# The start of the local layers: tile 0's shift column ahead of the table products, and tile 0's sine products and sum ahead of its power on POOL

## The chip, the cores and the metric

One core of a Trainium2 chip runs the whole program in one launch. The metric is the device time of an execution in microseconds; a profiled execution also gives a trace. The engines are TensorE (PE; PEld is its weight load), VectorE (DVE), ScalarE (ACT), GpSimd (POOL) and SyncE (SP), which here issues all DMAs. They work from queues of their own and meet by semaphores.

## The reference

The input x has 4 sequences of 1024 tokens with 128 features, in float32. The reference adds to x the normalised output of a latent attention (16 heads), and to the result the normalised output of a network of two "local layers", whose input is the normalised x. The change touches the first half of a local layer only:

```python
h = shift_token(x)                    # features 64..127 come from the token before
q, k, v = split(h @ wqkv)             # 8 heads of 64
q, k = l2norm(q) * qs, l2norm(k) * ksc
q = q * cos * scale + rotate_half(q) * sin * scale
k = k * cos / scale + rotate_half(k) * sin / scale
o = local_attention(q, k, v)          # windows of 64, this one and the one before
x = x + o @ wo
```

Behind it stands an MLP with a shift, a norm and a gate, and then the next layer, with other weights.

## The kernel before

**Stages.** `latent_attention_and_window_layers` calls `project`, `attend`, `mix`, then for each of the two layers `window` and `mlp`, and at the end `last_norm`. Each stage is a block in which every engine has a program of its own, written out in full; a new block starts when all engines have ended the last one. The residual stream `xf_sb` stays in SBUF throughout.

**`window`.** It works on 32 tiles (`NT`) of 128 tokens. `w_hT` holds a tile transposed, twice over, with one column more than tokens: its upper 64 partitions are written one column to the right, which makes the shift by a token, and column 0 of that half has to be filled from the last column of the tile before (times zero where a sequence starts). The function `carry` does this on DVE (L1120). For tile 0 it reads a column that a memset has set to zero.

**The path of a tile t.** TensorE turns it (`turn_x`, L891) and ScalarE copies it to `w_hT` in two pieces (L1001, L1003). TensorE projects queries and keys to PSUM (`project_qk`, L899) once copy and shift column are there, and values (`project_v`, L903). ScalarE copies queries and keys to `w_raw` (`copy_raw`, L1008) and squares them (L1013). DVE multiplies the PSUM values by the cosine table (`cosines`, L1134), and sums the squares by head (`sums`: L1125 and, with the floor, L1129, giving `w_ssm`). POOL makes the inverse root of these sums as a power with exponent -0.5 (`norms`, L1089, 128x16), and, in `rotate`, four products of `w_raw` with the sine table (L1079) and the sum of cosine and sine parts, `w_rot` (L1084). The norm commutes with the rotation, so DVE multiplies `w_rot` by the inverse roots at the end (`normalise`, L1143). TensorE turns the result (L911), ScalarE and DVE copy it to `w_qT` and `w_kT` (L1024, L1147), TensorE makes the scores (L917, L930), and so on through maxima (L1155), exponentials (L1031), division (L1168), turns, values (L954) and the output projection (L961).

**The order.** Each engine goes through slots s = -2 to 34, and in each slot does the steps of several tiles in an order written by hand (`slot`). In DVE's, the order is normalise(s-1), divide(s-2), carry(s+2), copy_kT(s-1), residual(s-3), cosines(s+1), maxima(s-1), copy_pT(s-2), maxima(s-1), sums(s+1). POOL has no slots: it does `norms` and `rotate` of each tile in turn. SP spreads the values of each tile with two DMAs (L877, L878), and starts with that after all four memsets.

**The start of a layer.** Before its first slot, DVE does four memsets (the shift column's source in `w_hT`, the left edges of `w_kT` and `w_vb0`, the floor of the square sums), which raise the semaphore `zeroed`, and six products that make the layer's cosine and sine tables from the given ones and the layer's scales (L1107, L1111), which raise `tables`. ScalarE waits for all four memsets before its first slot, POOL for all six products.

Of the kernel before, what the change touches and what calls it, by code (L numbers as in the profile page):

```python
# [20 lines left out]
ALU = mybir.AluOpType  # L21
# [4 lines left out]
P = 128  # L26
NT = B * S // P
TB = S // P
# [14 lines left out]
DEPTH, HEADS, DH, WIN = 2, 8, 64, 64  # L43
# [607 lines left out]
WINDOW_LOADS = 16 * (4 + 4 * DEPTH)  # L651
# [160 lines left out]
def window(nc, io, sb, layer):  # L812
# [6 lines left out]
    with ExitStack() as ctx:  # L819
# [7 lines left out]
        cos, sin = tile("w_cos", [P, TB, 2, DH]), tile("w_sin", [P, TB, 2, DH])  # L827
        hT = tile("w_hT", [P, 2, P + 1])
# [166 lines left out]
        def _(act):  # L995
# [67 lines left out]
                if runs(s - 2):  # L1063
                    copy_oT(s - 2, (s - 2) % 4)

            act.wait_ge(zeroed, layer * 4 + 4)
            slots(act, slot)

        @block.gpsimd
        def _(pool):  # L1070
            def rotate(t, r):

                at_least(pool, raw_done, base, t, 1)
                at_least(pool, rot_done, base, t, 0)
                out, src = (x.rearrange("p (w h u d) -> p w h u d", w=2, h=HEADS, u=2) for x in (t2[:, :], raw[:, r % 2, :]))
                for half in range(2):
                    for w in range(2):
                        tab = sin[:, t % TB, w, half * 32:half * 32 + 32].unsqueeze(1).broadcast_to((P, HEADS, 32))
                        i = pool.tensor_tensor(out[:, w, :, half, :], src[:, w, :, 1 - half, :], tab, ALU.mult)  # L1079
                i.then_inc(t2_done, 1)  # L1080
                at_least(pool, t1_done, base, t, 1)
                at_least(pool, t2_done, base, t, 1)
                at_least(pool, qkT_done, base, t, -1)
                pool.tensor_tensor(rot[:, r % 2, :], t1[:, r % 2, :], t2[:, :], ALU.add).then_inc(rot_done, 1)  # L1084

            def norms(t, r):
                at_least(pool, ssm_done, base, t, 1)
                at_least(pool, unit_done, base, t, -1)
                pool.tensor_tensor(rn[:, r % 2, :], ssm[:, r % 2, :], sb["mhalf"][:, 0:16], ALU.pow).then_inc(rn_done, 1)  # L1089

            pool.wait_ge(tables, layer * 6 + 6)
            for t in range(NT):
                norms(t, t % 4)
                rotate(t, t % 4)

        @block.vector
        def _(dve):

            dve.memset(hT[WIN:P, 1, P:P + 1], 0.0).then_inc(zeroed, 1)
            dve.memset(kT[:, :, :, 0:WIN], 0.0).then_inc(zeroed, 1)  # L1100
            dve.memset(vb[0][0:WIN, :], 0.0).then_inc(zeroed, 1)
            dve.memset(ss[:, :, :, 1], 1e-24).then_inc(zeroed, 1)

            dve.wait_ge(w_in, WINDOW_LOADS)
            for w in range(2):
                sc = sb["scales"][:, bass.ds(layer, 1), w, :].broadcast_to((P, TB, DH))
                dve.tensor_tensor(cos[:, :, w, :], sb["cos"][:, :, w, :], sc, ALU.mult).then_inc(tables, 1)  # L1107
                for half in range(2):
                    sc = sb["scales"][:, bass.ds(layer, 1), w, 32 - 32 * half:64 - 32 * half].broadcast_to((P, TB, 32))
                    part = slice(32 * half, 32 * half + 32)  # L1110
                    dve.tensor_tensor(sin[:, :, w, part], sb["sin"][:, :, w, part], sc, ALU.mult).then_inc(tables, 1)  # L1111
            dve.wait_ge(zeroed, layer * 4 + 4)
            dve.wait_ge(tables, layer * 6 + 6)

            def carry(t, r):

# [6 lines left out]
            def sums(t, r):  # L1123
                at_least(dve, sq_done, base, t, 1)
                dve.tensor_reduce(ss[:, r % 2, :, 0], sq[:, :].rearrange("p (h d) -> p h d", d=DH), AX.X, ALU.add).then_inc(ss_done, 1)  # L1125
                at_least(dve, ss_done, base, t, 1)
                at_least(dve, rn_done, base, t, -1)

                dve.tensor_reduce(ssm[:, r % 2, :], ss[:, r % 2, :, :], AX.X, ALU.max).then_inc(ssm_done, 1)  # L1129
# [44 lines left out]
            def slot(s):  # L1174
                def runs(t):
                    return 0 <= t < NT
                if runs(s - 1):
                    normalise(s - 1, (s - 1) % 4)
                if runs(s - 2):
                    divide(s - 2, (s - 2) % 4)  # L1180
                if runs(s + 2):
                    carry(s + 2, (s + 2) % 4)
                if runs(s - 1):
                    copy_kT(s - 1, (s - 1) % 4)
                if runs(s - 3):
                    residual(s - 3, (s - 3) % 4)
                if runs(s + 1):
                    cosines(s + 1, (s + 1) % 4)
                if runs(s - 1):
                    maxima(s - 1, (s - 1) % 4, 0)  # L1190
                if runs(s - 2):
                    copy_pT(s - 2, (s - 2) % 4)
                if runs(s - 1):
                    maxima(s - 1, (s - 1) % 4, 1)
                if runs(s + 1):
                    sums(s + 1, (s + 1) % 4)

            slots(dve, slot)

# [345 lines left out]
```

## Time and profile before

Three executions took 1448.87, 1451.42 and 1455.66 us; the median is 1451.42. The profiled execution took 1451.36 us, of which the traced span is 1449.6 us.

| Engine | busy us in the span | share |
|---|---|---|
| TensorE, matmuls | 1268.6 | 88% |
| DVE | 1129.5 | 78% |
| ScalarE | 930.0 | 64% |
| POOL | 705.3 | 49% |

| Stretch, us from the span's start | what runs | POOL busy us |
|---|---|---|
| 616 to 927 | `window` of layer 0 | 269.87 |
| 927 to 1020 | `mlp` of layer 0 | 9.66 |
| 1020 to 1331 | `window` of layer 1 | 269.98 |
| 1331 to 1422.9 | `mlp` of layer 1 | 9.66 |
| 1422.9 to 1449.6 | `last_norm` | 9.66 |

A profile's busy time is that in which an engine works on an instruction; waiting for a semaphore is idle time. The share of an engine over the whole span says little here, since POOL works in some stages only. A row of the timeline gives the start, the duration, the engine, the line, the operation with output and inputs, and in brackets the idle time before it with what ended it. The start of a row that shows no idle time can lie some hundredths of a microsecond before the end of the row before it on the same engine.

### The profile page before, as it was taken

How to read it: one execution, taken by the hardware profiler on the slowest of the kernel's cores; microseconds unless marked ns; L12 is line 12 of the kernel's file. 1: busy time of each engine (PE TensorE's matmuls, PEld its weight loads, DVE VectorE, ACT ScalarE, POOL GpSimd, SP SyncE). 2: the span in 40 equal slices, each digit the busy share in tenths (PEclk: the TensorE clock that was granted, in tenths of full speed). 3: DMA queues.
4: the chain of work that ended last, by engine and by line, in shares of the span. 5: the costliest groups of instructions: out<-in, count | busy, mean ns of one | idle time of the engine just before them, and what ended most of it. 6: DMA issues, size and time to landing. Idle time of an engine off the chain costs nothing. (4 is left out here: it accounts for less than half of the span.)

```text
span 1449.6 us, 30335 instructions
## 1 busy us (share of the span) xinstructions
PE 1268.6 (88%) x10501; PEld 718.9 (50%) x10501; DVE 1129.5 (78%) x2980; ACT 930.0 (64%) x2597; POOL 705.3 (49%) x742
## 2 busy tenths in 40 slices
PE   4689999999999997369999999699599999996991
PEld 2323333333343333336666666565366666665551
DVE  5788888888888861669899998566599989995667
ACT  4437777776777674748888887232488888883320
POOL 1011222122212221469999999110599999992102
PEclk9859999999999998579999999799899999998896
DMA  4431111111112002001211111000012111110001
GB/s 112 134 104 50 56 42 38 40 59 44 38 38 60 14 5 84 18 23 31 51 31 31 31 33 36 1 1 1 15 33 55 31 31 31 31 31 9 1 1 58
DMA packets 35055, 55.45 MB, mean 38 GB/s; under 512 B 6978, under 2 KB 22732, under 8 KB 32588
## 3 DMA queue, kind: packets, MB, share of 16 engines
q1 hardware_dynamic: 34328, 53.37, 14.0%
q8 instruction: 85, 1.39, 0.4%
q14 instruction: 66, 0.54, 0.1%
q10 hardware_dynamic: 576, 0.15, 0.1%
HBM read 26.77 MB, written 8.39 MB: 24 GB/s over the span
## 5 line engine op out<-in xcount | busy, mean ns | idle before, releaser
L516 ACT ACTIVATE a_prob<-a_psE 128x512 f32<-128x512 f32 (+3 forms) x768 | 318.3, 500 | 140.5 <-PE a_psE L444 137.9
L444 PE MATMUL a_psE<-a_qs,a_ks 84*128 84x512 bf16 (+3 forms) x768 | 248.3, 336 | 17.4 <-ACT a_prob L516 8.3
L599 DVE CUSTOM_DVE_ANT_0 a_psM<-a_psM,mask_q 128x384 f32<-128x384 f32 (+3 forms) x512 | 242.4, 507 | 18.6 <-PE a_psM L432 18.0
L432 PE MATMUL a_psM<-a_ks,a_qs 72*128 72x512 bf16 (+3 forms) x768 | 250.3, 343 | 5.7 <-PEq L86 3.2
L1089 POOL TENSOR_TENSOR w_rn<-w_ssm,mhalf 128x16 f32<-128x16 f32 x64 | 213.6, 3337 | 66.7 <-DVE w_ssm L1129 66.7
L551 POOL TENSOR_SCALAR_AFFINE_SELECT a_prob<-a_prob 128x512 f32<-128x512 f32 x128 | 81.1, 634 | 332.5 <-ACT a_prob L516 307.9
L601 DVE TENSOR_REDUCE a_nm<-a_psM 128x1 f32<-128x512 f32 x256 | 175.8, 687 | 46.6 <-PE a_psM L432 46.6
L1031 ACT ACTIVATE w_prob<-w_psS,w_bias 128x128 f32<-128x128 f32 x512 | 179.8, 376 | 21.4 <-DVE w_bias L1155 21.2
L1079 POOL TENSOR_TENSOR w_t<-w_raw,w_sin 128x256 f32<-128x256 f32 x256 | 178.6, 729 | 0.0
L444 PEld LDWEIGHTS a_psE<-a_qs,a_ks 84*128 84x128 bf16 x768 | 74.5, 98 | 180.3 <-ACT a_prob L516 97.1
L1084 POOL TENSOR_TENSOR w_rot<-w_t 128x1024 f32<-128x1024 f32 x64 | 150.9, 2358 | 8.8 <-issue 0.4
L458 PE MATMUL a_psO<-a_prob,v_all 128*32 128x512 f32 (+3 forms) x1536 | 148.4, 503 | 0.0
L899 PE MATMUL w_psQK<-w_wqkv,w_hT 128*128 128x512 f32 x256 | 124.1, 608 | 9.3 <-DVE w_t L1134 5.6
L1031 ACT ACTIVATION_READ_ACCUMULATOR w_prob<-w_psS,w_bias 128x1 f32 x512 | 110.6, 216 | 0.0
L1155 DVE TENSOR_REDUCE w_bias<-w_psS 128x4 f32<-128x512 f32 x128 | 87.7, 687 | 26.8 <-PE w_psS L930 26.8
L432 PEld LDWEIGHTS a_psM<-a_ks,a_qs 72*128 72x128 bf16 x768 | 76.4, 100 | 57.2 <-DVE a_nm L599 18.5
L1143 DVE TENSOR_TENSOR w_rot<-w_rot,w_rn 128x1024 f32<-128x1024 f32 x64 | 78.1, 1221 | 29.2 <-POOL w_rot L1084 29.2
L911 PE MATMUL w_psT<-ident,w_rot 128*128 128x128 f32 x512 | 70.8, 283 | 29.9 <-DVE w_rot L1143 27.1
L911 PEld LDWEIGHTS w_psT<-ident,w_rot 128*128 128x128 f32 x512 | 56.6, 144 | 75.5 <-DVE w_rot L1143 75.3
L1260 PE MATMUL f_psU<-f_hT,f_w 128*114 128x512 f32 (+1 forms) x192 | 88.8, 613 | 0.0
L1134 DVE TENSOR_TENSOR w_t<-w_psQK,w_cos 128x1024 f32<-128x1024 f32 x64 | 78.0, 1219 | 12.9 <-ACT w_raw L1008 12.7
L1038 ACT ACTIVATE w_pT<-w_psT 128x512 f32<-128x512 f32 x64 | 38.2, 598 | 73.4 <-PE w_psT L939 73.4
(136 smaller groups left out, 2371.5 us busy)
## 6 DMA issues: line engine op xcount, KB each, us to landing
w_vb<-w_v SPq DMA_DIRECT2D x128, 128.0 KB, 2.3
a_qs<-q_parts SPq DMA_DIRECT2D x16, 576.0 KB
a_ks<-k_parts SPq DMA_DIRECT2D x16, 576.0 KB
q_parts<-p_parts SPq DMA_DIRECT2D x24, 128.0 KB
k_parts<-p_parts SPq DMA_DIRECT2D x24, 128.0 KB
out_x<-l_y SPq DMA_DIRECT2D x8, 256.0 KB, 2.3
a_qs<-a_nmT SPq DMA_DIRECT2D x32, 48.0 KB
w_wqkv<-in_wqkv SPq DMA_DIRECT2D x2, 768.0 KB, 7.4
```

Source lines behind the costliest of these rows:

```text
L432: pe.matmul(out, qs[0:ROWS, g, j, i * P:(i + 1) * P], ks[0:ROWS, g, j, 512 * kc:512 * kc + n], start=True, stop=True).then_inc(m_ready, 1)
L444: pe.matmul(psE[:, r % NRING, 0:w], ks[0:KROWS, g, j, kt * P:(kt + 1) * P], qs[0:KROWS, g, j, q0:q0 + w], start=True, stop=True).then_inc( ...
L458: mm = pe.matmul(psO[32 * j:32 * j + 32, q0:512], v_flat[:, col + j * VA:col + j * VA + 32], prob[G % NPROB][:, j, 0:512 - q0], start=(kt ...
L516: act.activation(prob[G % NPROB][:, j, 0:w], psE[:, r % NRING, 0:w], ACT.Exp, scale=SCALE0).then_inc(e_read, 1)
L599: dve.tensor_tensor_reduce(scores, scores, sb["mask_q"][:, 512 - n:512], -1.0, -3.0 * NEG, ALU.add, ALU.min, low).then_inc(m_read, 1)
L601: dve.tensor_reduce(low, scores, AX.X, ALU.max, negate=True).then_inc(m_read, 1)
L899: pe.matmul(psQK[:, w, :], hT[:, r % 2, 0:P], wqkv[:, bass.ds(layer * (3 * INNER) + w * INNER, INNER)], start=True, stop=True).then_inc(qk ...
L911: i = pe.transpose(psT[:, w, c * P:(c + 1) * P], rot[:, r % 2, w * INNER + c * P:w * INNER + (c + 1) * P], sb["ident"])
L1031: i = act.activation(prob[:, p, w, c, :], psS[:, w, c * P:(c + 1) * P], ACT.Exp, bias=bias[:, p, n:n + 1], accum_out=den[:, p, n:n + 1])
L1079: i = pool.tensor_tensor(out[:, w, :, half, :], src[:, w, :, 1 - half, :], tab, ALU.mult)
L1084: pool.tensor_tensor(rot[:, r % 2, :], t1[:, r % 2, :], t2[:, :], ALU.add).then_inc(rot_done, 1)
L1089: pool.tensor_tensor(rn[:, r % 2, :], ssm[:, r % 2, :], sb["mhalf"][:, 0:16], ALU.pow).then_inc(rn_done, 1)
```

## The change

In both local layers:

- ScalarE starts its slots once one memset is done, not four.
- DVE does one memset (the source of the shift column), waits for it, and does the shift column of tile 0 at once; then the other three memsets and the six table products. Its slots follow, in which the column of tile 0 is left out.
- POOL does `rotate` of tile 0 first and `norms` of tile 0 after it. From tile 1 on it is `norms`, then `rotate`, as before.

Nothing that is computed changes.

```diff
-            act.wait_ge(zeroed, layer * 4 + 4)
+            act.wait_ge(zeroed, layer * 4 + 1)
             slots(act, slot)
...
             pool.wait_ge(tables, layer * 6 + 6)
-            for t in range(NT):
+            rotate(0, 0)
+            norms(0, 0)
+            for t in range(1, NT):
                 norms(t, t % 4)
                 rotate(t, t % 4)
...
-                if runs(s + 2):
+                if runs(s + 2) and s > -2:
                     carry(s + 2, (s + 2) % 4)
...
+            dve.memset(hT[WIN:P, 1, P:P + 1], 0.0).then_inc(zeroed, 1)
+            dve.wait_ge(zeroed, layer * 4 + 1)
+            dve.wait_ge(w_in, WINDOW_LOADS)
+            carry(0, 0)
+            dve.memset(kT[:, :, :, 0:WIN], 0.0).then_inc(zeroed, 1)
+            dve.memset(vb[0][0:WIN, :], 0.0).then_inc(zeroed, 1)
+            dve.memset(ss[:, :, :, 1], 1e-24).then_inc(zeroed, 1)
```

Behind these lines come the six products and the two waits on `zeroed` and `tables`, as they were; the whole piece stands behind the definitions of the steps now.

## Rows read from the trace of the kernel before

**Rows 1.** Mid-layer stretch: length, busy us of PE, PEld, DVE, ACT, POOL; clock, DMA.
```profile
662.80:680.50 17.70, 17.28 (x195) 11.96 (x194) 16.06 (x25) 14.74 (x49) 16.94 (x12) 1.00 0.13 31
```

**Rows 2.** Timeline of layer 1, middle: start, duration, engine, line, operation.
```profile
1190.11 1.22 DVE L1143 TENSOR_TENSOR w_rot<-w_rot,w_rn 128x1024 f32<-128x1024 f32 x1
1190.27 3.82 POOL L1089 TENSOR_TENSOR w_rn<-w_ssm,mhalf 128x16 f32<-128x16 f32 x1 [0.54 <-DVE w_ssm L1129]
...
1199.30 2.91 POOL L1089 TENSOR_TENSOR w_rn<-w_ssm,mhalf 128x16 f32<-128x16 f32 x1
1199.45 1.23 DVE L1143 TENSOR_TENSOR w_rot<-w_rot,w_rn 128x1024 f32<-128x1024 f32 x1 [0.70 <-POOL w_rot L1084]
```

**Rows 3.** Timeline of the start of layer 0.
```profile
616.28 0.45 PE L891 MATMUL w_psT<-ident,xf_sb 128*128 128x128 f32 x1 [14.35 <-PEq L686]
616.30 0.06 DVE L1099 MEMSET w_hT<- 64x1 f32 x1 [2.04 <-PEq L686]
...
617.62 0.27 ACT L1001 ACTIVATE w_hT<-w_psT 64x128 f32<-64x128 f32 x1 [1.65 <-DVE w_ss L1102]
...
618.24 0.48 PE L891 MATMUL w_psT<-ident,xf_sb 128*128 128x128 f32 x1 [1.51 <-ACT w_hT L1003]
...
620.21 0.34 DVE L1120 TENSOR_SCALAR w_hT<-w_hT,carry 64x1 f32<-64x1 f32 x2
...
620.57 3.75 PE L899 MATMUL w_psQK<-w_wqkv,w_hT 128*128 128x512 f32 x4 [1.86 <-DVE w_hT L1120]
...
624.36 1.02 ACT L1008 ACTIVATE w_raw<-w_psQK 128x1024 f32<-128x1024 f32 x1 [3.29 <-PE w_psQK L899]
...
625.42 1.22 DVE L1134 TENSOR_TENSOR w_t<-w_psQK,w_cos 128x1024 f32<-128x1024 f32 x1 [4.87 <-ACT w_raw L1008]
...
626.79 1.95 PE L899 MATMUL w_psQK<-w_wqkv,w_hT 128*128 128x512 f32 x4 [1.10 <-DVE w_t L1134]
...
627.80 0.19 DVE L1129 TENSOR_REDUCE w_ssm<-w_ss 128x16 f32<-128x32 f32 x1
...
628.14 2.90 POOL L1089 TENSOR_TENSOR w_rn<-w_ssm,mhalf 128x16 f32<-128x16 f32 x1 [14.07 <-DVE w_ssm L1129]
...
631.00 2.77 POOL L1079 TENSOR_TENSOR w_t<-w_raw,w_sin 128x256 f32<-128x256 f32 x4
...
633.86 1.02 ACT L1008 ACTIVATE w_raw<-w_psQK 128x1024 f32<-128x1024 f32 x1 [1.91 <-POOL w_t L1079]
633.92 2.34 POOL L1084 TENSOR_TENSOR w_rot<-w_t 128x1024 f32<-128x1024 f32 x1
636.22 2.91 POOL L1089 TENSOR_TENSOR w_rn<-w_ssm,mhalf 128x16 f32<-128x16 f32 x1
636.36 1.22 DVE L1143 TENSOR_TENSOR w_rot<-w_rot,w_rn 128x1024 f32<-128x1024 f32 x1 [3.96 <-POOL w_rot L1084]
...
644.94 1.22 DVE L1143 TENSOR_TENSOR w_rot<-w_rot,w_rn 128x1024 f32<-128x1024 f32 x1
```

**Rows 4.** Timeline of the start of layer 1.
```profile
1028.14 1.02 ACT L1008 ACTIVATE w_raw<-w_psQK 128x1024 f32<-128x1024 f32 x1 [3.07 <-PE w_psQK L899]
...
1040.14 1.23 DVE L1143 TENSOR_TENSOR w_rot<-w_rot,w_rn 128x1024 f32<-128x1024 f32 x1 [3.95 <-POOL w_rot L1084]
...
1048.26 1.23 DVE L1143 TENSOR_TENSOR w_rot<-w_rot,w_rn 128x1024 f32<-128x1024 f32 x1
```

**Rows 5.** TensorE in stretches: busy, granted clock, DMA share, GB/s.
```profile
620.00:625.00 5.00, 4.43 (x6) 0.50 0.00 0
625.50:635.00 9.50, 5.06 (x12) 1.00 0.24 55
636.00:642.00 6.00, 4.34 (x39) 0.50 0.00 0
```

**Rows 6.** Timeline of layer 0's end: the normalisations of tiles 30 and 31.
```profile
902.46 1.23 DVE L1143 TENSOR_TENSOR w_rot<-w_rot,w_rn 128x1024 f32<-128x1024 f32 x1 [0.72 <-POOL w_rot L1084]
...
911.12 1.22 DVE L1143 TENSOR_TENSOR w_rot<-w_rot,w_rn 128x1024 f32<-128x1024 f32 x1
```

More of the change, by code:

```diff
@@ L1097, in _ @@
         def _(dve):
[L1099 to L1113, printed above, removed]
             def carry(t, r):
@@ L1196, in slot @@
                     sums(s + 1, (s + 1) % 4)
+            dve.memset(hT[WIN:P, 1, P:P + 1], 0.0).then_inc(zeroed, 1)
[5 more added lines that the diff above has]
+            dve.memset(ss[:, :, :, 1], 1e-24).then_inc(zeroed, 1)
+            for w in range(2):
+                sc = sb["scales"][:, bass.ds(layer, 1), w, :].broadcast_to((P, TB, DH))
+                dve.tensor_tensor(cos[:, :, w, :], sb["cos"][:, :, w, :], sc, ALU.mult).then_inc(tables, 1)
+                for half in range(2):
+                    sc = sb["scales"][:, bass.ds(layer, 1), w, 32 - 32 * half:64 - 32 * half].broadcast_to((P, TB, 32))
+                    part = slice(32 * half, 32 * half + 32)
+                    dve.tensor_tensor(sin[:, :, w, part], sb["sin"][:, :, w, part], sc, ALU.mult).then_inc(tables, 1)
+            dve.wait_ge(zeroed, layer * 4 + 4)
+            dve.wait_ge(tables, layer * 6 + 6)
             slots(dve, slot)
```

## The prediction

> **What bounds the kernel now.** The kernel is a row of stages with a meeting of all engines between them, so I first cut the span by stage. The two window layers last some 311 us each, from 616.3 and from 1020.2. The chain of waits of the page covers only the last norm, behind the last such meeting, and says nothing of the layers; their order has to be read from the timeline.
>
> In the middle of a layer two tiles take 17.70 us and POOL is busy for 16.94 of them [rows 1]. POOL does three things per tile: the power (2.91 or 3.82 us) [rows 2], four sine products (2.77) and the sum (2.34) [rows 3]. Each even tile's power waits 0.54 us for the square sums that DVE has only just made; an odd one's starts at once [rows 2]. In return every second normalisation on DVE waits 0.70 us for POOL's sum. So POOL and DVE hold each other, and neither has slack that could swallow a late start or an early one: what the first tile gains should stay to the layer's last tile.
>
> Call N(t) the start of DVE's normalisation of tile t. It is the first thing DVE does in a slot, and TensorE's turns, the scores and the exponentials of the slot hang on it. In the middle of a layer N steps by 9.34 us from odd to even (1190.11 to 1199.45), and by 8.40 from even to odd, since two steps make the 17.7 us pair [rows 1, 2].
>
> The start of a layer is where the change sits [rows 3]. TensorE has turned tile 0 at 616.73, but ScalarE begins its copy at 617.62, put down to DVE's last memset. The next turn ends at 618.72, and TensorE then waits for DVE's shift column: it stands behind the memsets and the six table products, starts at 620.21, and lets the query and key projection start at 620.57. The raw copy follows at 624.36, the squares' sum and maximum end at 627.99, and only at 628.14 does POOL do its first piece, tile 0's power. Its sine products start at 631.00, 5.6 us after the raw tile lay there, and N(0) is 636.36. Layer 1 has the same distances: raw copy at 1028.14, N(0) at 1040.14, again 12.00 us later [rows 4].
>
> **The change, part by part.**
>
> *ScalarE's shorter wait.* It waits for one memset, which ends at 616.36, not four. Its first copy can start when the turn ends, at 616.73 + 0.05 = 616.78, not 617.62. The second turn followed the copy's start by 0.62 us, so it runs from 617.40 to 617.88. Nobody reads the three other memsets before DVE itself passes them in program order, or SP before its first spread of V, which needs V's copy, several us later.
>
> *The shift column of tile 0 first.* It adds one wait of DVE on its own memset, and moves one instruction, half of the 0.34 us pair [rows 3]: it is over by 616.8, so the projection starts behind the second turn, at about 617.90 instead of 620.57. Gain 2.67 us. The projection takes the same 3.75 us, at the low granted clock of 0.50 [rows 5], and ends at 621.65; the raw copy runs from 621.69 to 622.71. Queued behind the moved column are three memsets and six products. They end some 0.3 us later, near 620.5, and tile 1's column near 620.7. Nothing waits: the cosines of tile 0 need the raw tile of 622.71. That column and wait cost nothing while that cover of 2 us lasts. The cover for POOL's wait on the tables is the same.
>
> *POOL's new order for tile 0.* Sine products, sum, power. The sine products need the raw tile and the tables: from 622.8, 2.77 us, to 625.6. The sum starts 0.15 later and ends at 625.72 + 2.34 = 628.06. It needs the cosines, which DVE makes from 622.75 to 623.97 (raw copy plus 1.22): there. The power starts at 628.0; the maximum of the square sums is ready by 622.71 + 2.61 = 625.3 (before: 625.38 to 627.99): there. It ends at 630.92, and N(0) waits for it instead of for the sum: about 631.0. Gain of N(0): 636.36 - 631.0 = 5.35 us, of which 2.67 is the column's and 2.7 the order's (POOL no longer waits from the raw tile's end at 625.38 to 628.14). The work of POOL is the same, 8.0 us; it only begins earlier.
>
> *Who else is queued behind it.* ScalarE's raw copy of tile 2 waits for tile 0's sine products, which now end at 625.6 instead of 633.8: harmless. Is DVE free at 631.0? Tile 1: its projection may start when tile 0's cosines are done, 624.0, takes 1.95 (the same form at 626.79), and its raw copy runs 626.05 to 627.07; squares' maximum 2.61 later, 629.7. That is 1.2 us ahead of 630.9, when POOL wants it for tile 1's power. If TensorE were still at half clock there, the projection would take 3.9 us and POOL would lose 0.7. Tile 2's raw copy starts near 630.4, when before it was 633.86; its reader, DVE's third cosine piece, comes four us behind N(0). So what stands around N(0) is late by less than it was early.
>
> *What comes after N(0).* Before, POOL starts tile 1's power at 636.22 and DVE its normalisation at 636.36, both let go by the sum. After, both are let go by tile 0's power, at 630.9 and 631.0. The order on both engines from there is untouched.
>
> *The sum.* 5.35 us in layer 0 and the same in layer 1, as its distances are the same: 10.7 us. The profiled execution took 1451.36 us, 1.8 over its span and 0.1 below the median of 1451.42. The median less 10.7 is 1440.7, down 0.74%. About 0.5% (7.3 us) is what a measurement of this kernel can tell from no change.
>
> **A cost that the trace shows elsewhere.** The power takes 3.82 us when DVE's normalisation has begun just before it (1190.11, then 1190.27), and ends 2.76 us after that normalisation ends; it takes 2.91 when POOL is first by 0.15 (1199.30, then 1199.45) [rows 2]. So POOL's read is held off while DVE reads two SBUF operands. In the new start POOL's second power is queued on POOL itself and DVE's normalisation hears a semaphore, so I expect POOL first, as at 636.22; but the lead of 0.14 us there follows a sum, and behind a power the trace has no such pair. Bounds: nothing lost, or 1 us a layer as in rival 1. I take nothing, the nearer row.
>
> The Trainium skill has this lock (SBUF — State Buffer, "SBUF: two separate sides"): the instruction that starts first, if VectorE's reads two SBUF inputs against a GpSimd one, keeps the shared pair to its end and the other stands still. The blocked power agrees; the other half does not, since the normalisation that starts 0.15 behind a power takes 1.23 and not 2.9 us more. By the rule both kernels would lose alike there, and the sum would stay.
>
> **Rivals.**
>
> *1. The normalisation wins the lock at tile 1 (0.18).* The power of tile 1 is then the long one: N(1) is N(0) + 9.34 instead of + 8.58 (636.36 to 644.94), or + 8.12 in layer 1 [rows 3, 4]. From there odd and even change roles. The next step is 8.40 for 9.34, so most of it is back two tiles on, but the layer's last step, N(30) to N(31), becomes 9.34 where it is 8.66 now [rows 6]. Layer 0 loses 0.76 - 0.94 + 0.68 = 0.5, layer 1, whose first step was 0.46 shorter, 1.0. Gain 10.7 - 1.5 = 9.2, time 1442.2. For it: both events are released by one instruction. The rule of the skill cited above says who suffers here, not who is first.
>
> *2. TensorE keeps its clock (0.15).* Before, it stood idle before N(0)'s turns and fell to the low level, 0.50 from 636 to 642, after 1.00 until 635 [rows 5]. After, the idle time is 630.3 to 632.3, half as long. If the clock stays at 1.00, DVE's slot no longer ends last; then POOL's 8.1 us does, and N(1) is N(0) + 8.2. The next power then starts before N(1), and odd and even change roles one step later, which is worth up to the 0.94 by which the steps differ, less 0.68 at the layer's end. Layer 0: 0.4 + 0.94 - 0.68 = 0.7; layer 1, whose first step is short already, 0.2. Gain 11.6, time 1439.8.
>
> *3. Half is lost (0.08).* One part frees POOL but the other is held by something the trace does not show, such as tile 1's sums late by over 2 us, so only the column's 2.67 or the order's 2.7 a layer arrives: 5.3 us, 1446.1. Against it are the 1.2 us and 2 us of cover above.
>
> *4. Nothing happens (0.04).* ScalarE or TensorE still starts late, or a layer's end is not tied to its start. 1451. Against it: POOL is idle for 0.76 us in 17.70 [rows 1].
>
> *5. Slower (0.05).* Every power becomes a long one. That needs DVE to be ready for the next normalisation before each power, so its slot would have to beat POOL's 9.3 us and still be first at every tile. Each step would be 9.34 instead of 8.87 on average: 0.47 x 31 x 2 = 29 us more, less 10.7: 1470. It decides at the point where POOL waits for the square sums at every tile; today it waits at each second one, and after a long power POOL is the late one, which corrects it. So it is unlikely.
>
> **How the numbers follow.** The forecast has 0.50, and its time is 1440.7. Faster by over 0.5%: forecast, rivals 1 and 2, 0.83. Within 0.5%: rivals 3 and 4, 0.12. Slower: 0.05. The range takes in rivals 1 and 2 and, on either side, some 2 us by which a median of these runs (1448.87 to 1455.66) may stand off: 1436.5 to 1444.5; the 0.17 of rivals 3 to 5 stay outside.
>
> **What would show it.** The timeline of the changed kernel: the first projection at 1.6 to 1.7 us after the first turn (now 4.3), at once behind the second turn. POOL's first instruction of a layer a sine product, 6.5 us after the first turn and 0.1 behind the raw copy; the power with no idle time before it. N(0) 14.7 us after the first turn instead of 20.1, put down to POOL's power. The last normalisation of each layer about 5.3 us nearer to the layer's start, and the MLPs and the last norm unchanged in length. Tile 1's power 2.91 us if the forecast holds, 3.8 to 4.0 for rival 1; the clock between N(0) and N(1) for rival 2. The prediction is wrong if N(31) - N(0) grows by over 2 us, or if POOL idles between its power of tile 0 and that of tile 1.

## The result, and the profile after

The changed kernel took 1444.21 us (median of 4 executions, 1443.88 to 1445.37), the kernel before 1453.24 on the same chip (4, 1448.87 to 1455.66): ratio 0.9945, 95% interval 0.9921 to 0.9969. Two repeats, with more executions beside them, gave 0.9946 (0.9930 to 0.9962) and 0.9936 (0.9913 to 0.9958). It is faster by 8 to 9 us where 10.7 were forecast, and 1444.2 stands 3.5 us over the forecast time of 1440.7. The forecast started from a median of 1451.4 in three executions, and the same kernel's median is 1453.2 in four: by that alone the forecast time would be 1442.5, and 1.7 us are left.

The page of the changed kernel's profiled execution (1445.37 us), its span and two groups:

```profile
span 1443.6 us, 30337 instructions
...
L1089 POOL TENSOR_TENSOR w_rn<-w_ssm,mhalf 128x16 f32<-128x16 f32 x64 | 213.7, 3340 | 16.7 <-DVE w_ssm L1115 16.7
...
L1079 POOL TENSOR_TENSOR w_t<-w_raw,w_sin 128x256 f32<-128x256 f32 x256 | 178.7, 731 | 39.3 <-ACT w_raw L1008 39.3
```

Before, POOL's power had 66.7 us of idle time ahead of it and the sine products none: POOL now comes to a layer's first tile with the sine products. Line numbers have moved: normalise is L1129, the shift column L1106, the square sums' maximum L1115, the cosines L1120.

The start of layer 0, timeline of the changed kernel (start, duration, engine, line), beside [rows 3]:

```profile
620.18 0.45 PE L891 MATMUL w_psT<-ident,xf_sb 128*128 128x128 f32 x1 [14.35 <-PEq L686]
620.21 0.06 DVE L1184 MEMSET w_hT<- 64x1 f32 x1 [2.04 <-PEq L686]
620.30 0.21 DVE L1106 TENSOR_SCALAR w_hT<-w_hT,carry 64x1 f32<-64x1 f32 x1
...
620.73 0.27 ACT L1001 ACTIVATE w_hT<-w_psT 64x128 f32<-64x128 f32 x1 [0.85 <-PE w_psT L891]
...
621.60 3.62 PE L899 MATMUL w_psQK<-w_wqkv,w_hT 128*128 128x512 f32 x4
...
625.26 1.02 ACT L1008 ACTIVATE w_raw<-w_psQK 128x1024 f32<-128x1024 f32 x1 [2.85 <-PE w_psQK L899]
...
626.43 2.78 POOL L1079 TENSOR_TENSOR w_t<-w_raw,w_sin 128x256 f32<-128x256 f32 x4 [8.46 <-ACT w_raw L1008]
...
629.36 2.35 POOL L1084 TENSOR_TENSOR w_rot<-w_t 128x1024 f32<-128x1024 f32 x1
...
631.67 5.78 POOL L1089 TENSOR_TENSOR w_rn<-w_ssm,mhalf 128x16 f32<-128x16 f32 x2
...
634.61 1.23 DVE L1129 TENSOR_TENSOR w_rot<-w_rot,w_rn 128x1024 f32<-128x1024 f32 x1 [1.31 <-POOL w_rn L1089]
```

The column lies right behind its memset, the projection starts 1.4 us behind the first turn (4.3 before), POOL begins with the sine products 0.15 us behind the raw copy, and N(0) stands 14.40 us behind the first memset, 20.06 before. The powers of tiles 0 and 1 take 5.78 us together: 2.9 each, neither is blocked.

The layer as a whole is best read from a few distances. N(t) is the start of DVE's normalisation of tile t, as in the prediction; M is the layer's first memset, E the first memset of the MLP behind it. All are from the timelines of the profiled executions, in us. Rows below those of the two repeats belong to the experiments, which come later; "filled" are those with added turns on TensorE.

| Kernel, layer | N(0)-M | N(1)-N(0) | N(2)-N(1) | N(30)-N(0) | N(31)-N(30) | E-N(31) | E-M |
|---|---|---|---|---|---|---|---|
| before, 0 | 20.06 | 8.58 | 9.35 | 266.10 | 8.66 | 17.07 | 311.89 |
| before, 1 | 19.84 | 8.12 | 9.36 | 265.66 | 8.69 | 17.07 | 311.26 |
| changed, 0 | 14.40 | 8.17 | 8.12 | 264.52 | 9.31 | 18.51 | 306.74 |
| changed, 1 | 13.87 | 8.16 | 9.28 | 266.03 | 9.59 | 18.51 | 308.00 |
| repeat, 0 | 14.42 | 8.17 | 9.21 | 265.60 | 9.31 | 18.54 | 307.87 |
| repeat, 1 | 13.91 | 8.18 | 9.29 | 266.00 | 9.61 | 18.53 | 308.05 |
| second repeat, 0 | 14.10 | 8.17 | 9.31 | 265.75 | 9.31 | 18.44 | 307.60 |
| second repeat, 1 | 13.88 | 8.19 | 9.26 | 266.06 | 9.59 | 18.53 | 308.06 |
| column alone, 0 | 16.57 | 8.12 | 9.34 | 265.70 | 8.68 | 17.33 | 308.28 |
| column alone, 1 | 16.54 | 8.11 | 9.35 | 265.04 | 9.60 | 19.11 | 310.29 |
| order alone, 0 | 17.25 | 8.18 | 9.37 | 265.74 | 9.31 | 18.46 | 310.76 |
| order alone, 1 | 17.20 | 8.18 | 9.37 | 265.75 | 9.60 | 18.40 | 310.95 |
| memset at tile 4, 0 | 14.41 | 8.18 | 9.20 | 266.60 | 8.66 | 16.86 | 306.53 |
| memset at tile 4, 1 | 14.04 | 8.18 | 9.35 | 266.13 | 9.31 | 18.41 | 307.89 |
| before, memset at tile 5, 0 | 20.07 | 8.11 | 8.27 | 264.50 | 9.31 | 18.20 | 312.08 |
| before, memset at tile 5, 1 | 20.06 | 8.10 | 8.41 | 264.62 | 9.31 | 19.05 | 313.04 |
| filled, slot 32, 0 | 14.41 | 8.18 | 8.12 | 264.59 | 9.33 | 15.63 | 303.96 |
| filled, slot 32, 1 | 14.28 | 8.18 | 9.20 | 265.98 | 9.60 | 16.69 | 306.55 |
| filled, slots 32, 33, 0 | 14.41 | 8.18 | 8.11 | 264.55 | 9.34 | 15.64 | 303.94 |
| filled, slots 32, 33, 1 | 13.75 | 8.18 | 9.21 | 266.00 | 9.62 | 15.63 | 305.00 |
| filled, slots 2, 32, 33, 0 | 14.40 | 8.18 | 8.12 | 264.43 | 9.33 | 15.63 | 303.79 |
| filled, slots 2, 32, 33, 1 | 12.99 | 9.33 | 8.11 | 265.93 | 9.61 | 15.63 | 304.16 |

N(0) comes 5.6 to 6.0 us earlier in a layer, and the two stages together are only 7.2 to 8.4 us shorter. From N(0) on, the layer has become longer by 0.5 to 1.7 us (layer 0) and 2.7 to 2.8 us (layer 1). Behind N(30) alone it is 2.0 to 2.4 us longer in every one of these layers; in layer 0 the stretch from N(0) to N(30) has become shorter, in layer 1 longer by 0.3 to 0.4. The rest of the span is outside the change: the instructions ahead of layer 0 are the same, and yet M of layer 0 lay between 613.9 and 620.2 us in the profiled executions. The profile that was predicted from had 616.3, the changed kernel's 620.2; that is why the spans differ by only 6.0 us although the two stages are 8.4 shorter.

### The profile page after: what moved, and what is told of

It reads as the page before. It is cut to its first block and busy times, and to the rows that moved or that the text cites. A ratio compares the mean times of both kernels' runs of the same rounds, so it can differ in the third digit from the quotient of the medians.

```text
span 1443.6 us, 30337 instructions
## 1 busy us (share of the span) xinstructions
PE 1267.0 (88%) x10501; PEld 717.8 (50%) x10501; DVE 1129.8 (78%) x2980; ACT 930.5 (64%) x2597; POOL 705.5 (49%) x742
## 3 DMA queue, kind: packets, MB, share of 16 engines
HBM read 26.77 MB, written 8.39 MB: 24 GB/s over the span
## 5 line engine op out<-in xcount | busy, mean ns | idle before, releaser
L432 PEld LDWEIGHTS a_psM<-a_ks,a_qs 72*128 72x128 bf16 x768 | 76.4, 100 | 57.1 <-DVE a_nm L599 18.5
L1129 DVE TENSOR_TENSOR w_rot<-w_rot,w_rn 128x1024 f32<-128x1024 f32 x64 | 78.2, 1221 | 29.7 <-POOL w_rot L1084 27.1
L899 PEld LDWEIGHTS w_psQK<-w_wqkv,w_hT 128*128 128x128 f32 x256 | 49.2, 194 | 68.4 <-issue 68.4
```

The costliest lines, as they stand in the source:

```text
L432: pe.matmul(out, qs[0:ROWS, g, j, i * P:(i + 1) * P], ks[0:ROWS, g, j, 512 * kc:512 * kc + n], start=True, stop=True).then_inc(m_ready, 1)
L899: pe.matmul(psQK[:, w, :], hT[:, r % 2, 0:P], wqkv[:, bass.ds(layer * (3 * INNER) + w * INNER, INNER)], start=True, stop=True).then_inc(qk ...
```

## The experiments

Two theories were held against each other. **"Roles"**: the start gain arrives in full, and the layer's end takes part of it back, since the long power (3.82 us, DVE's normalisation ahead of it) has passed from even to odd tiles [rows 2, 6]. **"Wear"**: the gain is used up along the layer. The "long power" is the one of 3.82 us; a tile "has" it when its own power is the long one.

### Each part alone

```diff
  # "column": the changed kernel with POOL's old order
-            rotate(0, 0)
-            norms(0, 0)
-            for t in range(1, NT):
+            for t in range(NT):
```

> The changed kernel with POOL's old order for tile 0 (power first): the column's part alone. Both theories: the first projection starts 2.7 us earlier, the raw copy, POOL's power and N(0) too, so N(0) stands 17.4 us behind the layer's first memset (before 20.06 and 19.84, changed kernel 14.40 and 13.87). Theory 'roles' (a start gain arrives in full, and a layer's end takes some 2.1 us back if the long power has passed from even to odd tiles): nothing makes POOL's first steps other than in the kernel before, but TensorE's idle time before the first normalisation is as long as there, so even tiles keep the long power, the end from N(31) to the next stage is 17.07 us and each window stage is 2.7 us shorter, 5.4 in all: ratio 0.996. Theory 'wear' (a start gain is used up along the layer whatever the order): the stages are less than 2 us shorter and the loss stands between N(1) and N(30).

```diff
  # "order": the kernel before with POOL's new order for tile 0
-            for t in range(NT):
+            rotate(0, 0)
+            norms(0, 0)
+            for t in range(1, NT):
```

> The kernel before with tile 0's sine products and sum in front of its power: the order's part alone. Both: the raw copy stays where it was, N(0) comes 2.7 to 2.9 us earlier, 17.2 us behind the first memset. Theory 'roles': TensorE stands idle for 2 us before N(0)'s turns as in the changed kernel, keeps its clock, N(1) comes 8.2 us behind N(0), the long power passes to odd tiles at least in layer 0, and the step N(30) to N(31) is 9.3 and the end 18.5 us there: the stage is 2.7 + 0.4 + 0.9 - 2.1 = about 2 us shorter. If the even tiles keep it, 2.8 us. Ratio 0.996 to 0.998. Theory 'wear': under 2 us in both layers whoever has the long power.

Timelines of layer 0; M is 616.95 with the column alone, 614.31 with the order alone. First the column's:

```profile
625.31 2.90 POOL L1089 TENSOR_TENSOR w_rn<-w_ssm,mhalf 128x16 f32<-128x16 f32 x1 [10.59 <-DVE w_ssm L1113]
...
633.52 1.22 DVE L1127 TENSOR_TENSOR w_rot<-w_rot,w_rn 128x1024 f32<-128x1024 f32 x1 [3.95 <-POOL w_rot L1084]
```

The order's:

```profile
623.38 2.77 POOL L1079 TENSOR_TENSOR w_t<-w_raw,w_sin 128x256 f32<-128x256 f32 x4 [11.31 <-ACT w_raw L1008]
...
631.56 1.23 DVE L1145 TENSOR_TENSOR w_rot<-w_rot,w_rn 128x1024 f32<-128x1024 f32 x1 [1.30 <-POOL w_rn L1089]
```

N(0)-M is 16.5 to 16.6 with the column, 0.8 better than expected, and 17.2 with the order, as expected. The column's surplus is TensorE's: its first projection took 3.15 us in layer 0 of this run, 3.75 before. Ratios: column 0.9973 (0.9957 to 0.9990), order 0.9985 (0.9969 to 1.0001). By stages, the column gives 3.6 and 1.0 us, the order 1.1 and 0.3. The column was expected to give 5.4 in all and gave 4.6; the order, expected at 2 to 2.8 a layer, gave less, and its interval reaches 1, so by times alone it cannot be told from no change. The table shows where the difference to N(0)'s gain went: layer 0 of the column kept the long power on even tiles and has an end of 8.68 + 17.33; the other three layers ended with it on the odd ones, at 27.8 to 28.7 us from N(30) to E, where layer 0 of the column has 26.0 and the kernel before 25.7 to 25.8. Against "wear": N(30) - N(0) is 265.0 to 265.8 us in all four, and 265.7 to 266.1 in the kernel before.

The roles can also pass late. In layer 1 of the column's run the steps alternate in the old way to tile 28; then one is 8.71 instead of 8.39, and from there the order is turned. In layer 1 of the changed kernel the same step has 0.35 us too much (9.69 for 9.34): DVE stands idle though POOL's sum is done. What holds it there is open. This step is too long by 0.3 us or more in layer 1 of every kernel of these runs that has the moved column and keeps POOL's old order from tile 1 to tile 30, and in neither layer of the kernels without the moved column; so it comes with that part of the change.

### The changed kernel again

> The changed kernel once more, as the measure for the others of this call and for how much the stages ahead of the first window stage differ from one profiled execution to the next. Both theories: window stages 306.7 and 308.0 us. If the 3.9 us by which the first window stage began later in the changed kernel's profile are chance, this one begins within 616 to 621 at another place.

> The changed kernel on the same chip as the two others of this call, as their measure. Layer stages 306.7 to 308.1 us, ends of 18.5 us.

M of layer 0 was 618.4 and 618.8, the stages 307.9 and 308.1, then 307.6 and 308.1 us. In both, N(2) - N(1) is 9.2 to 9.3 in both layers, where the first profile had 8.12 in layer 0. So the first profile shows the better of two courses there.

### Passing the long power back

```diff
             for t in range(1, NT):
+                if t == 2:
+                    pool.memset(pspare[:, :], 0.0)
                 norms(t, t % 4)
```

> The changed kernel with one more POOL instruction, a memset of 128x512 to a tile that nobody reads, between tile 1's sum and tile 2's power, in both layers. It delays the power of tile 2 by about 0.4 us, so that the normalisation of tile 1 is first. Theory 'roles': tile 2's power then takes 3.8 to 4.2 us instead of 2.91, N(2) comes about 9.4 us behind N(1) (changed kernel 8.12 and 9.28), the long power stays with the even tiles to the end, the step N(30) to N(31) is 8.66 instead of 9.31 and 9.59, and from N(31) to the next stage 17.07 us instead of 18.51. Added work makes the kernel faster: layer 0 by 2.1 - 1.25 = 0.9 us, layer 1 by about 2.4 - 0 = 2.4 us, in sum 3 us below the changed kernel. Theory 'wear': the added work costs 0.4 to 1.6 us a layer and the end stays at 18.5 us.

This missed: the end stayed at 18.4 and the ratio was 0.9952 (0.9933 to 0.9971). The added memset did make tile 2's power long (3.67 us), but N(2) to N(3) was long too, 9.33 us, so that the alternation came out as without it. The step behind N(1) was 9.2 to 9.3 in the changed kernel already, since DVE's slot and not POOL set it. The cause is in the clock, below. The second attempt put the memset where the steps had settled:

```diff
             for t in range(1, NT):
+                if t == 4:
+                    pool.memset(pspare[:, :], 0.0)
                 norms(t, t % 4)
```

> The changed kernel with one more POOL instruction, a memset of 128x512 to a tile that nobody reads (0.52 us where it was tried before), this time ahead of tile 4's power, where the steps have settled (before, ahead of tile 2's, both engines still ran through TensorE's low clock and the long power fell on tile 3 as well). Theory 'roles' (a layer's end costs 2.1 us more when odd tiles have the long power): tile 4's power becomes long, N(3) to N(4) is 9.35 instead of 8.39, and from there even tiles have the long power: N(30) to N(31) 8.7 instead of 9.3 to 9.6, from N(31) to the next stage 17.1 to 17.3 us instead of 18.5. The stage is 1.0 us longer ahead and 2.1 shorter behind: about 306.8 us against 307.9 in layer 0 and 308.0 in layer 1, in spite of added work. Theory 'wear': the added work costs 0.5 to 1.5 us a layer and the end stays at 18.5: 308.5 to 309.5 us.

Timeline of layer 0 with it, tile 4 and the layer's end:

```profile
656.51 0.53 POOL L1097 MEMSET w_pspare<- 128x512 f32 x1
656.68 1.23 DVE L1132 TENSOR_TENSOR w_rot<-w_rot,w_rn 128x1024 f32<-128x1024 f32 x1 [0.70 <-POOL w_rot L1085]
657.00 3.68 POOL L1090 TENSOR_TENSOR w_rn<-w_ssm,mhalf 128x16 f32<-128x16 f32 x1
...
666.04 1.23 DVE L1132 TENSOR_TENSOR w_rot<-w_rot,w_rn 128x1024 f32<-128x1024 f32 x1 [0.89 <-POOL w_rot L1085]
...
905.21 1.22 DVE L1132 TENSOR_TENSOR w_rot<-w_rot,w_rn 128x1024 f32<-128x1024 f32 x1
...
922.07 0.54 DVE L1358 MEMSET f_last<- 128x576 f32 x1 [0.47 <-PEq L819]
```

The normalisation starts 0.3 us ahead of the power, the power takes 3.68 us, and the step is 9.36 instead of 8.39. At the other end N(31) to E is 16.86 us where the changed kernel had 18.5, and N(30) to N(31) 8.66 where it had 9.31. The stage is 306.53 us, 1.1 to 1.3 below the two repeats, with half a microsecond of work added on POOL. (The changed kernel's first profile has 306.74 there, but with the short step behind N(1), 8.12; here that step was 9.20.) "Wear" is out for this layer. In layer 1 the steps alternated in the way of before up to tile 28, then came 8.72 for 8.39, and the end was the long one again, 9.31 + 18.41. The ratio 0.9947 (0.9928 to 0.9966) cannot tell 1 us from nothing; the timeline does.

The converse, on the kernel before:

```diff
             for t in range(NT):
+                if t == 5:
+                    pool.memset(pspare[:, :], 0.0)
                 norms(t, t % 4)
```

> The kernel before with one more POOL instruction, the memset of 128x512 to a tile that nobody reads, between tile 4's sum and tile 5's power: the converse of the run that put it ahead of tile 4's power in the changed kernel. Theory 'roles': it makes tile 5's power the long one, N(4) to N(5) is 9.35 instead of 8.39, and from there odd tiles have it: N(30) to N(31) 9.3 instead of 8.66, from N(31) to the next stage 18.5 instead of 17.07. 0.5 us of added work cost 0.95 + 0.65 + 1.44 = 3 us a layer: stages of 314.9 and 314.3 us against 311.9 and 311.3, 6 us in all, ratio 1.004. Theory 'no roles' (the changed kernel's long ends come from its other start in another way): 0.5 to 1 us a layer and an end of 17.07.

This missed too. In the profiled execution the steps of layer 0 began 8.11, 8.27, 9.34 and not 8.58, 9.35, 8.38 as in the kernel before: the odd tiles had the long power before the memset was reached, and the memset filled a time in which POOL would have waited for the square sums. The ends, from N(30) to E, were 27.5 and 28.4 us, as wherever the odd tiles have it, and the stages 312.1 and 313.0. So the run does not price a turn in mid-layer; it shows that the kernel before can come into either course by itself. The ratio was 1.0000 (0.9986 to 1.0015).

### TensorE's clock at the layer's end

```diff
  # "warm": s == NT; "warm2": s in (NT, NT + 1); at the start of TensorE's slot
+                if s in (NT, NT + 1):
+                    at_least(pe, raw_done, base, NT - 1, 1)
+                    at_least(pe, t1_done, base, NT - 1, 1)
+                    for _ in range(16):
+                        pe.transpose(psQK[:, 0, 0:P], sb["ident"], sb["ident"])
```

> The changed kernel with 16 turns of the identity into a free PSUM bank, whose results nobody reads, that TensorE makes at the start of its second last but two slot, ahead of the turns of tile 31, in both layers. It tells what of the layer's longer end is TensorE's low granted clock. Theory 'roles': N(30) to N(31) stays 9.3 to 9.6, as POOL sets it; TensorE no longer stands idle for 3.3 us, so its clock stays 1.00, the eight turns take 1.09 instead of 1.97 and the output projection 1.06 instead of 1.61, and from N(31) to the next stage it is 17.1 us or less instead of 18.5: stages of about 306.5 us. Rival (the end is longer for another cause, the order of DVE's and ScalarE's steps): the end stays at 18.4 or more whatever the clock.

> The changed kernel with 16 turns of the identity, whose results nobody reads, at the start of TensorE's slots 32 and 33, in both layers; the run with those of slot 32 alone had ends of 15.63 and 16.69 us, and in the second TensorE's clock fell while it waited 2.15 us for ScalarE. Theory 'roles and clock': both ends are 15.6 us, 2.9 below the changed kernel's 18.5, layer stages of 304 to 305.5 us, and the kernel is 6 to 8 us below the changed one: 1437 to 1439 us, ratio 0.990. Rival: the second filling delays the output projection of tile 30, 0.5 to 1 us worse than slot 32 alone.

The changed kernel at the end of layer 0, timeline:

```profile
899.13 1.22 DVE L1129 TENSOR_TENSOR w_rot<-w_rot,w_rn 128x1024 f32<-128x1024 f32 x1
899.29 3.82 POOL L1089 TENSOR_TENSOR w_rn<-w_ssm,mhalf 128x16 f32<-128x16 f32 x1 [0.53 <-DVE w_ssm L1115]
...
908.44 1.23 DVE L1129 TENSOR_TENSOR w_rot<-w_rot,w_rn 128x1024 f32<-128x1024 f32 x1 [2.20 <-POOL w_rot L1084]
...
909.72 1.97 PE L911 MATMUL w_psT<-ident,w_rot 128*128 128x128 f32 x8 [3.34 <-DVE w_rot L1129]
...
911.48 1.61 PE L961 MATMUL w_psO<-w_wo,w_oT 128*128 128x128 f32 x8
```

Its TensorE in two stretches (length, busy, granted clock, DMA):

```profile
899.00:908.00 9.00, 5.84 (x91) 1.00 0.13 31
908.50:912.50 4.00, 2.78 (x13) 0.59 0.00 0
```

The kernel before at the same place:

```profile
909.00:915.00 6.00, 4.74 (x67) 1.00 0.01 3
922.00:924.00 2.00, 2.00 (x16) 0.50 0.04 8
```

With slots 32 and 33 filled, timeline:

```profile
900.06 1.97 PE L971 MATMUL w_psQK<-ident 128*128 128x128 f32 x16
903.49 1.09 PE L911 MATMUL w_psT<-ident,w_rot 128*128 128x128 f32 x8 [1.46 <-DVE w_rot L1134]
904.42 1.06 PE L961 MATMUL w_psO<-w_wo,w_oT 128*128 128x128 f32 x8
```

and its TensorE:

```profile
903.20:908.00 4.80, 4.51 (x60) 1.00 0.00 0
```

Tile 31's power is the long one, so DVE waits 2.20 us for POOL and TensorE 3.34 us for DVE; then TensorE's eight turns take 1.97 us and the projection 1.61, at half clock. Filled, they take 1.09 and 1.06. N(31) to E falls from 18.5 to 15.63 (layer 0) and 16.69 (layer 1) with slot 32 alone, and to 15.64 and 15.63 with slot 33 too, below the 17.07 of the kernel before. In that kernel TensorE was at half clock in one stretch of the end, near 922, behind 2.14 us of waiting for ScalarE; in the changed kernel in two, and with both slots filled in none: 17.07, 18.51 and 15.63. N(30) to N(31) stays 9.3 to 9.6: that part is POOL's. So both added microseconds of the end have their cause: 0.65 to 0.9 from the long power, 1.44 from the clock. Slot 32 alone ran at 1440.03 us, ratio 0.9914 (0.9889 to 0.9938); both at 1439.03, 0.9910 (0.9892 to 0.9927).

### The low clock at the layer's start

Layer 1 of the changed kernel, timeline of the slot behind N(1):

```profile
1039.94 1.23 DVE L1129 TENSOR_TENSOR w_rot<-w_rot,w_rn 128x1024 f32<-128x1024 f32 x1 [1.11 <-POOL w_rot L1084]
...
1041.22 1.09 PE L911 MATMUL w_psT<-ident,w_rot 128*128 128x128 f32 x8 [2.25 <-DVE w_rot L1129]
...
1044.11 1.88 PE L930 MATMUL w_psS<-w_kT,w_qT 64*64 64x128 f32 x32
...
1049.22 1.22 DVE L1129 TENSOR_TENSOR w_rot<-w_rot,w_rn 128x1024 f32<-128x1024 f32 x1
```

TensorE there:

```profile
1033.08:1034.78 1.70, 1.51 (x10) 1.00 0.00 0
1034.50:1038.00 3.50, 3.06 (x39) 1.00 0.00 0
1038.00:1041.50 3.50, 1.25 (x6) 1.00 0.02 5
1042.50:1045.00 2.50, 2.43 (x22) 0.50 0.31 71
1046.00:1048.00 2.00, 2.00 (x37) 1.00 0.00 0
```

The clock is 1.00 for tile 0's turns (1033.07 on), as rival 2 had it, and falls one slot later, behind the 2.25 us in which TensorE waits for N(1). The scores take 1.88 us instead of 1.10, and the step is 9.28 instead of 8.12. In layer 0 of the same execution TensorE waited the same 2.25 us and the clock stayed at 1.00: that is the short step of 8.12. What decides between the two is open. In the kernel before, the low clock fell into the slot before [rows 5], where it cost at most 0.4 us. A last kernel fills this place too:

```diff
+                if s == 2:
+                    for _ in range(16):
+                        pe.transpose(psO[:, 0:P], sb["ident"], sb["ident"])
```

> The kernel with the fillings of slots 32 and 33, and 16 turns of the identity more at the start of slot 2, ahead of the turns of tile 1, in both layers. In the changed kernel TensorE stands idle for 2.2 us there, its clock falls to 0.50 in the slot, and the step from N(1) to N(2) is 9.2 to 9.3 us in seven of the eight layers seen with both parts of the change, 8.12 in the others. Theory 'the low clock has moved by one slot': with the filling the clock stays 1.00, the step is 8.1 us in both layers, N(30) - N(0) 264.5 us instead of 265.6 to 266.0, the long power stays with the odd tiles, and the layers are 1.1 to 1.5 us shorter than with slots 32 and 33 alone: stages of 304 us in both (warm2: 303.94, where the step was short by chance, and 305.00). Rival (DVE or ScalarE sets the step): it stays at 9.2 in at least one layer, with the clock at 1.00.

(Of all layers run with both parts and nothing added at the start, N(2) - N(1) was short (8.1) in 3 and long (9.2 to 9.35) in 11; the count in the expectation was of too few.) The step was 8.12 and 8.11, the stages 303.79 and 304.16 us, N(30) - N(0) 264.43 in layer 0 but 265.93 in layer 1. There the first projection ran at the full clock from the start. Timeline of layer 1, M at 1010.04:

```profile
1011.19 1.89 PE L899 MATMUL w_psQK<-w_wqkv,w_hT 128*128 128x512 f32 x4
1013.12 1.02 ACT L1016 ACTIVATE w_raw<-w_psQK 128x1024 f32<-128x1024 f32 x1 [1.17 <-PE w_psQK L899]
1014.33 2.77 POOL L1087 TENSOR_TENSOR w_t<-w_raw,w_sin 128x256 f32<-128x256 f32 x4 [29.47 <-DVE w_sin L1206]
...
1015.96 3.49 PE L899 MATMUL w_psQK<-w_wqkv,w_hT 128*128 128x512 f32 x4 [1.91 <-DVE w_t L1128]
```

The projection takes 1.89 us, and the prediction's cover is gone: POOL waits for the sine tables, DVE's cosines stand behind them, TensorE waits and makes the second projection at half clock, and tile 1's power is the long one (N(1) - N(0) 9.33). N(0) is still 12.99 us behind M, and the layer is as short as layer 0. This kernel took 1436.27 us (6 executions, 1432.01 to 1439.71), ratio 0.9897 (0.9874 to 0.9921), the shortest of all. The intervals of the three filled kernels overlap; the order among them is shown by their stages only.

### POOL's new order elsewhere

```diff
  # "allrot": every tile; in "last" tile 31 alone, tiles 1 to 30 as they were
-            for t in range(1, NT):
-                norms(t, t % 4)
-                rotate(t, t % 4)
+            for t in range(NT):
+                rotate(t, t % 4)
+                norms(t, t % 4)
```

> The changed kernel with POOL's new order for tile 31 too: sine products and sum, then the power. In the changed kernel tile 31's power waits 0.53 us for the square sums and 0.9 for DVE's normalisation of tile 30, and N(31) waits 2.2 us for POOL. Theory 'roles': the sine products start 0.4 us before N(30); if DVE's normalisation holds them for up to 1.2 us, the power ends 7.9 to 9.1 us behind N(30) and N(31) is 0.2 to 1.4 us earlier than now (9.3); with less idle time on TensorE the end may fall to 17.1: stages 0.3 to 2.8 us shorter than 307.9. Theory 'wear': no change within 0.3 us.

> The changed kernel with the new order, sine products, sum, power, for every tile and not for tile 0 alone. Theory 'free POOL': the power no longer starts beside a normalisation and POOL no longer waits for the square sums, so POOL needs 8.1 us a tile; DVE's slot of 8.39 sets the step at every tile: 8.4 instead of 8.87 on average, 14 us a layer, 1416 us in all. Theory 'lock': the sine products and the sum read two SBUF operands for far longer than the power, so that now DVE's normalisation and division (1.23 us each) hold up POOL, or POOL holds up them, at every tile: POOL needs 8.1 + 1.2 to 2.4 us, the step is 9.3 to 10.5 us at every tile and the kernel 27 to 100 us slower than the changed one.

For tile 31 alone nothing was won: N(30) to N(31) 9.90 and 9.64 us, ratio 0.9952 (0.9936 to 0.9969). Its sine products took 4.75 us instead of 2.78. For every tile it was 1518.03 us, ratio 1.0460 (1.0434 to 1.0487), with a step of 10.09 us at every tile. Groups of layer 0, count, busy, mean ns, first in the changed kernel over its whole stage:

```profile
L1079 POOL TENSOR_TENSOR w_t<-w_raw,w_sin 128x256 f32<-128x256 f32 x128 | 89.3, 731 | 8.5 <-ACT w_raw L1008 8.5
...
L1129 DVE TENSOR_TENSOR w_rot<-w_rot,w_rn 128x1024 f32<-128x1024 f32 x32 | 39.1, 1222 | 14.6 <-POOL w_rot L1084 13.3 <-POOL w_rn L1089 1.3
```

and with the new order for every tile, over the stretch 616 to 930 us, which holds 30 or so of the 32 tiles:

```profile
L1079 POOL TENSOR_TENSOR w_t<-w_raw,w_sin 128x256 f32<-128x256 f32 x124 | 144.3, 1195 | 8.5 <-ACT w_raw L1008 8.5
...
L1127 DVE TENSOR_TENSOR w_rot<-w_rot,w_rn 128x1024 f32<-128x1024 f32 x30 | 52.2, 1740 | 33.0 <-POOL w_rn L1089 33.0
L1152 DVE TENSOR_TENSOR w_prob<-w_prob,w_rden 128x1024 f32<-128x1024 f32 x29 | 44.2, 1525 | 1.0
```

The power ends, DVE starts the normalisation and POOL the next sine products, both with two SBUF operands. POOL's four products grow by 1.9 us, the normalisation by 0.5 and the division (1.22 before) by 0.3. The cosines, whose other operand lies in PSUM, take their 1.22 us beside POOL's sum in this kernel too. For tile 0 the order costs nothing: POOL goes on with tile 1's power and not with sine products, the two powers take 5.78 us together, and the normalisation beside them 1.23. The Trainium skill (SBUF — State Buffer, "SBUF: two separate sides") says that the instruction that starts first keeps the shared ports and the other one stands still. The theory "lock" had sign and size right (a step of 9.3 to 10.5 us, measured 10.09). The rows add that against a row of short POOL instructions both sides lose.

## Why the prediction was right or wrong, point by point

- **The start, right.** N(0) was forecast 5.35 us earlier, and came 5.6 to 6.0. The order's share was forecast at 2.7 and measured at 2.6 to 2.8; the column's, 2.67, at 3.3 to 3.5; in the column's run the first projection took 3.15 to 3.25 us, where 3.75 was assumed. ScalarE's first copy, the projection, POOL's first instruction and the releaser of N(0) are where they were put. The cover of POOL's wait on the tables held in every run of the changed kernel itself and was gone in the one where TensorE had its full clock.
- **The two powers, right.** POOL was first at tile 1 in all layers of the changed kernel: rival 1 did not happen as told.
- **The sum, wrong in one step.** The step that failed is "what the first tile gains should stay to the layer's last tile". It stays until about N(30): N(30) - N(0) moved by -1.6 to +0.4. But the layer's end was taken as fixed. The long power had passed to the odd tiles, and behind N(30) the layer is 2.1 us longer (layer 0) and 2.3 (layer 1). The prediction's own sign of being wrong, N(31) - N(0) longer by over 2 us, did not show this: that distance moved by -0.9 and +1.3, since most of the loss lies behind N(31).
- **Why the roles passed.** Rival 2 had the place and the direction right and only half of the mechanism. TensorE did keep its clock for tile 0's turns (it had waited 1.84 us for them, before 4.48), N(1) - N(0) fell to 8.17, and tile 2's power was first. But the low clock was not gone; in most layers it came one slot later and cost 1.1 us there, where rival 2 expected 0.9 us of gain. That the clock is what passed the roles is argued and not shown. In all eight layers of the changed kernel, its two repeats and the order alone, DVE waits 1.1 us for POOL's sum at N(1). In the column alone, with the low clock, DVE does not wait, but starts only 0.01 to 0.07 us ahead of POOL's next power; and in the kernel before with a memset at tile 5, also with the low clock, it waits 0.18 to 0.19 us and the roles pass. With the low clock it is a close race. No run filled TensorE's wait ahead of N(0) and nothing else.
- **The end was priced too low.** Rivals 1 and 2 counted 0.68 us for a last step on an odd tile. The other 1.44 us, TensorE idle for 3.34 us behind it and then at half clock, were in neither. Put in afterwards, 0.65 + 1.44 and 0.9 + 1.44 for 0.68, with rival 2's 0.94 left out, would have made its sum 5.35 + 5.35 + 0.4 - 2.1 - 2.35 = 6.7 us, and with the start as measured 7.6, where the stages gave 7.2 to 8.4.
- **The level.** The stages give 7.2 to 8.4 us, the medians 8.0 to 9.0. That 1444.21 still lies inside the stated 1436.5 to 1444.5, by 0.3 us, is partly luck: the start gave 0.9 to 1.2 us more in the two layers than forecast, and that made up for part of the 4.4 us lost at the two ends. The two MLPs together took 182.1 to 183.2 us in three profiles of the changed kernel and 183.6 in that of before; what of that is chance was not separated.
- **Rival 5** did not occur with this change. The nearest to it is the new order for every tile, where not the power but the sine products were held at every tile, and the kernel was 4.6% slower.

## What to carry to other kernels

A gain at the start of a pipelined stage is not safe because the middle of the stage is full: look at who is first where the engines alternate, and follow the last tile to the stage's end under either order. Where TensorE waits two to three microseconds for a single producer near such an end, count what it does after the wait at the low clock too; a few unused turns there were worth 1.8 to 2.9 us a layer, more than the choice of POOL's order for tile 0 (1.1 and 0.3). An exchange of two instructions that pays for one tile can cost at every tile, if it puts two instructions with two SBUF operands on DVE and POOL side by side.

## What the runs showed of the hardware

- A memset of 0.5 us on POOL, 26 tiles ahead of a layer's end, made the end 2.3 us shorter in layer 0, through an alternation with a period of two tiles (8.39 and 9.34 us) that the tiles in between passed on.
- POOL's power against DVE's normalisation: 2.91 us when POOL is 0.14 us ahead, 3.82 when 0.16 behind, 3.68 when 0.3 behind; DVE's instruction takes 1.22 to 1.23 in each case. Against sine products DVE's takes 1.74, and the four products 4.75 instead of 2.78.
- After an idle time of 2.25 us TensorE went back to work at full clock. In layer 1 of the changed kernel the clock fell to 0.50 some 1.1 us later, in layer 0 of its first repeat 0.2 us later, with the order alone 1.3 us later, and in layer 0 of the changed kernel not at all. After 3.34 us it was at half clock at once in layer 0 of the changed kernel, and 0.7 us later in layer 0 of the order alone. The same wait does not cost the same twice.
- M of layer 0, behind 614 to 620 us of unchanged instructions, scattered by 6 us from one profiled execution to another; a change of 8 us can only be followed by distances inside its stage.
